# Attention burst of weighted values in two halves, and score maxima per PSUM bank

## The reference

```python
scores = jnp.einsum('bsqhd,bthd->bqhst', qh, kh) * scale
probs = jax.nn.softmax(scores, axis=-1)
a_dot = jnp.einsum('bqhst,bthd->bsqhd', probs, vh)
a_mem = sigma_q @ memory / (sigma_q @ memory_norm)   # sigma_q = elu(q)
out = a_dot * (1.0 - w) + a_mem * w
```

## Time and profile before

| | before |
|---|---|
| median of three runs | 767.34 us |
| profiled execution | 764.37 us |
| its span, first to last instruction | 762.6 us |
| PE busy | 705.8 us (93%) |
| DVE busy | 587.5 us (77%) |
| ACT busy | 486.2 us (64%) |
| POOL busy | 133.7 us (18%) |

### The profile page before, as it was taken

The page is one execution under the profiler, slowest core; times in us unless marked ns, Lnnn a source line. Parts: engine busy times, 40 slices in busy tenths (PEclk is TensorE's granted clock), DMA queues, the critical chain, the costliest instruction groups (busy, mean ns, idle before and its releaser), DMA issues.

```text
span 762.6 us, 14199 instructions
## 1 busy us (share of the span) xinstructions
PE 705.8 (93%) x3976; PEld 374.4 (49%) x3977; DVE 587.5 (77%) x800; ACT 486.2 (64%) x886; POOL 133.7 (18%) x282
## 2 busy tenths in 40 slices
PE   4999999898888888999988888899999999999998
PEld 2456544522222222221222212378888888888887
DVE  5366488899998899899899984377778777767754
ACT  1473600388888888888888878655665665556332
POOL 1000000666531111111111111010000000004750
PEclk9999999999999999999999999999999999999999
DMA  9729100187411110011110172042111111122431
GB/s 314 255 69 315 62 0 1 40 255 240 121 46 32 32 32 25 24 32 32 32 27 22 46 248 102 22 130 63 44 54 55 51 45 55 55 93 75 125 113 46
DMA packets 49951, 65.35 MB, mean 86 GB/s; under 512 B 8168, under 2 KB 42880, under 8 KB 49920
## 3 DMA queue, kind: packets, MB, share of 16 engines
q1 hardware_dynamic: 38560, 40.58, 16.8%
q10 hardware_dynamic: 8288, 15.99, 6.4%
q0 software_dynamic: 3072, 8.39, 3.5%
HBM read 40.15 MB, written 24.38 MB: 85 GB/s over the span
## 4 chain that ended last, share of the span: by engine, by line
PE 76%; ACT 11%; issue 5%; DVE 5%; ACTq 1%; DMA 1%; SPq 1%; POOL 0%; DVEq 0%; POOLq 0%
PE ps L1373 14%; PE ps L1402 14%; ACT att L736 10%; PE ps L1426 9%; PE ps L1472 9%; PE ps L1256 8%; PE ps L1506 6%; DVE smax L1006 4%; PE ps L1248 3%; PE ps L1521 3%; PE ps L1463 2%; PE ps L1216 2%; PE ps L1281 1%; PE ps L1362 1%; PE ps L1213 1%
## 5 line engine op out<-in xcount | busy, mean ns | idle before, releaser
L1006 DVE TENSOR_REDUCE smax<-ps 128x2 f32<-128x1024 f32 x256 | 302.4, 1221 | 33.6 <-PE ps L1281 30.5
L736 ACT ACTIVATE att<-ps 128x512 f32<-128x512 f32 x512 | 267.8, 602 | 53.6 <-PE ps L1426 50.8
L1426 PE MATMUL ps<-att 51*128 51x512 bf16 x512 | 165.4, 382 | 33.4 <-ACT att L736 21.0
L1281 PE MATMUL ps<-att 48*128 48x512 bf16 x512 | 163.0, 384 | 1.4 <-DVE smax L1006 1.4
L1426 PEld LDWEIGHTS ps<-att 51*128 51x128 bf16 x512 | 39.7, 93 | 200.9 <-ACT att L736 94.0
L1373 PE MATMUL ps<-att,v_head 128*32 128x512 f32 x1024 | 136.4, 604 | 1.7 <-ACT o_sb L695 0.6
L1402 PE MATMUL ps<-att_r 128*128 128x512 f32 x456 | 119.2, 410 | 2.8 <-DVE att_r L1067 2.8
L1063 DVE TENSOR_TENSOR att_r<-big,att_r 128x1024 fp32r<-128x1024 f32 x76 | 90.4, 1229 | 24.4 <-ACT att_r L716 23.8
L1402 PEld LDWEIGHTS ps<-att_r 128*128 128x128 f32 x456 | 86.7, 191 | 22.2 <-DVE att_r L1067 3.3
L716 ACT ACTIVATE att_r<-big 128x1024 fp32r x74 | 74.3, 1052 | 18.7 <-issue 18.7
L1472 PE MATMUL ps<-big,xn 128*128 x312 | 73.7, 380 | 0.0
(11 more groups left out here) (165 smaller groups left out, 697.0 us busy)
## 6 DMA issues: line engine op xcount, KB each, us to landing
big<-w ACTq DMA_DIRECT2D x8, 1024.0 KB
q_stacks<-big SPq DMA_DIRECT2D x12, 512.0 KB
att<-q_stacks SPq DMA_DIRECT2D x64, 96.0 KB, 2.1
slot_x<-zeros SPq DMA_DIRECT2D x1, 4992.0 KB, 17.1
e_x<-slot_x SPq DMA_DIRECT2D x39, 128.0 KB, 2.0
slot_y<-xn SPq DMA_DIRECT2D x39, 128.0 KB, 1.7
big<-w ACTq DMA_DIRECT2D x8, 512.0 KB
att<-k_stacks SPq DMA_DIRECT2D x64, 48.0 KB, 2.0
```

What stands on the lines that cost most here:

```text
L736: act.activation(probs[:, t % 2, g, :], ps[:, RING[turn_of(u) % 3], :], ACT.Exp, scale=SCALE)\
L1006: dve.reduce_max(smax[:, s % 2, :].rearrange("p (half v) -> p half v", half=2)[:, :, v], ps[:, bank:bank + 2, :], X_AXIS).then_inc(max_don ...
L1281: return pe.matmul(ps[:, bank + half, :], q_st[s][rows, g, P * st:P * (st + 1)], k_st[s][rows, :], start=True, stop=True)
L1426: pe.matmul(ps[:, RING[turn % 3], :], k_st[s][rows, P * t:P * (t + 1)], q_st[s][rows, g, :], start=True, stop=True).then_inc(scores_ready, 1)
```

## The change

The weighted values are split by their 512 queries into two parts of 256. The first part stands behind the quarter's first score pair (g = 0), the second behind the other one. The waits for the exponentials, for the values and for the copy of the previous outputs stand before the first part. The accumulation starts with part 0 and ends with part 1. The transposed outputs stand between the second pair and the second part.

The maxima are taken by two instructions for each tile, one for each bank, the bank of half 1 first, which is the one that PE writes first. Semaphores `a_ready` and `max_done` count banks, 16 per step, instead of tiles. On PE each `max_scores` matmul waits for its own bank. The hidden maxima of the shared stage do the same.

```diff
+        PART = SEQ // 2
...
-                pool.wait_ge(max_done, i * 8 + 8)
+                pool.wait_ge(max_done, i * 16 + 16)
...
 
             def maxima(i, s, v, bank):
 
-                dve.wait_ge(a_ready, i * 8 + (v + 1))
                 if v == 0:
                     wait(dve, m_ready, i - 1)
-                dve.reduce_max(smax[:, s % 2, :].rearrange("p (half v) -> p half v", half=2)[:, :, v],
-                               ps[:, bank:bank + 2, :], X_AXIS).then_inc(max_done, 1)
+                for half in (1, 0):
+                    dve.wait_ge(a_ready, i * 16 + (2 * v + 2 - half))
+                    dve.reduce_max(smax[:, s % 2, 8 * half + v:8 * half + v + 1], ps[:, bank + half, :], X_AXIS)\
+                       .then_inc(max_done, 1)
 
             res(1, kf, kr, kc[0])
 
...
                 bank = 2
                 if v == 0:
                     pe.wait_ge(stack_loaded[s], blk * 64 + 64)
-                wait(pe, max_done, i * 8 + v)
-                for half in range(2):
-                    last = max_scores(s, v, half, bank)
-                last.then_inc(a_ready, 1)
+                for half in (1, 0):
+                    wait(pe, max_done, i * 16 + (2 * v - half))
+                    max_scores(s, v, half, bank).then_inc(a_ready, 1)
 
             def max_scores(s, v, half, bank):
                 g, st = divmod(v, ST)
...
-                    pe.wait_ge(max_done, 16)
+                    pe.wait_ge(max_done, 32)
...
                                         o_sb[:, a, P * st:P * (st + 1)], ident[:, :])
                 last.then_inc(oT_in_psum, 1)
 
-            def weighted_values(i, s, t, pair=0):
-                pe.wait_ge(probs_ready, i * 16 + 4 * (t + 1))
-                if t == 0:
-                    pe.wait_ge(v_head_ready, i + 1)
-                    if s % 2 == 0:
-                        wait(pe, o_copied, pair)
+            def weighted_values(i, s, t, part, pair=0):
+
+
+                if part == 0:
+                    pe.wait_ge(probs_ready, i * 16 + 4 * (t + 1))
+                    if t == 0:
+                        pe.wait_ge(v_head_ready, i + 1)
+                        if s % 2 == 0:
+                            wait(pe, o_copied, pair)
+                queries = slice(PART * part, PART * (part + 1))
                 for g in range(G):
-                    last = pe.matmul(ps[32 * g:32 * (g + 1), 6, :], v_head[:, s % 2, t, :], probs[:, t % 2, g, :],
-                                     start=s % 2 == 0 and t == 0, stop=s % 2 == 1 and t == ST - 1)
-                last.then_inc(pv_done, 1)
+                    last = pe.matmul(ps[32 * g:32 * (g + 1), 6, queries], v_head[:, s % 2, t, :],
+                                     probs[:, t % 2, g, queries], start=s % 2 == 0 and t == 0 and part == 0,
+                                     stop=s % 2 == 1 and t == ST - 1 and part == 1)
+                if part == 1:
+                    last.then_inc(pv_done, 1)
 
             def transpose_x(j, pair, a):
                 pe.wait_ge(ex_loaded[a], pair * 16 + 16)
...
                             rows = slice(HALF * half, HALF * half + RM)
                             if not (last and turn - 3 == MAX_AT):
                                 bank_free(i, turn, pair if s % 2 == 0 else 0)
-                            if ahead and half == 0:
-                                if v == 0:
+                            if ahead:
+                                if v == 0 and half == 0:
                                     pe.wait_ge(stack_loaded[(s + 2) % 4], (blk + (s + 2) // 4) * 64 + 64)
-                                if isinstance(i, int) and i == 0 and v < 2:
+                                if isinstance(i, int) and i == 0 and v < 2 and half == 0:
                                     pe.wait_ge(mem_used, NT // 2 - 1 + v)
-                                wait(pe, max_done, (i + 2) * 8 + (v - 1))
+                                wait(pe, max_done, (i + 2) * 16 + (2 * v + half - 3))
                             pe.matmul(ps[:, RING[turn % 3], :], k_st[s][rows, P * t:P * (t + 1)],
                                       q_st[s][rows, g, :], start=True, stop=True).then_inc(scores_ready, 1)
                             if ahead:
-                                ins = max_scores((s + 2) % 4, v, 1 - half, 2 * (v % 2))
-                                if half == 1:
-                                    ins.then_inc(a_ready, 1)
-                    if t == OUT_AT // G - 1 and s % 2 == 0 and not first:
-                        transpose_o(pair - 1, (s // 2 + 1) % 2)
-
-                    if t > 0:
-                        weighted_values(i, s, t - 1, pair)
-                    elif not first:
-                        weighted_values(i - 1, s + 3, ST - 1)
+                                max_scores((s + 2) % 4, v, 1 - half, 2 * (v % 2)).then_inc(a_ready, 1)
+                        if t == OUT_AT // G - 1 and g == PAIR - 1 and s % 2 == 0 and not first:
+                            transpose_o(pair - 1, (s // 2 + 1) % 2)
+                        if t > 0:
+                            weighted_values(i, s, t - 1, g, pair)
+                        elif not first:
+                            weighted_values(i - 1, s + 3, ST - 1, g)
                     if t == MAX_AT // G - 1 and not last:
                         transpose_max(i + 1, s + 1)
 
...
                     step(blk, s)
             for i in range(STEPS - 4, STEPS):
                 step(NLOOP - 1, i % 4, ahead=i + 2 < STEPS, last=i == STEPS - 1)
-            weighted_values(STEPS - 1, STEPS - 1, ST - 1)
+            for part in range(2):
+                weighted_values(STEPS - 1, STEPS - 1, ST - 1, part)
             def transpose_h(j, a):
                 pe.wait_ge(h_ready, j + 1)
                 wait(pe, hT_ready, j)
```

## The result

Before and after in six runs each: 766.92 us (763.16 to 767.78) and 757.67 us (756.18 to 758.52). The ratio is 0.9882 [0.9864, 0.9901]: 9.25 us or 1.2% faster. The forecast was 757.6. The profiled execution of the kernel after took 757.83 us (span 755.7), 6.5 less than that of before; the latter lay 2.6 under its median, at a mean granted clock of 0.998. Of 35 executions of that kernel beside the experiments, the 15 at 0.998 took 764.2 to 766.0 us and the 18 at 0.993 to 0.996 took 766.3 to 769.1.

A forecast was written before the change was run, and what follows sets the result against it. A ring of PE and ACT was taken as the bound. Fourteen pairs at 0.66 (9.2) plus 0.9 less 0.4 gave 9.7 us: 764.37 to 754.7 profiled, 757.6 as median with 2.97 added; 8-in-10 range 747 to 771.

The forecast's parts named there:

- The ring: Ordinary quarter before: PE and ACT wait for each other, with the whole weighted-values block in the chain, 2.47 us a quarter.
- DVE 2.6 from being the bound: Pair of steps before: DVE's work makes 18.6 of 21.23 us, so DVE loses 2.6 us and does not bound.
- Half burst, 0.88: Weighted values on PE: 0.88 us between score pairs around one half, 0.25 of it per entry; PE's quarter 2.20 us.
- Reductions, 0.60 apart: Maxima on DVE: reductions of 512 elements 0.60 us apart, 0.06 of it the price of an instruction.
- The rival at 0.68: Neighbouring 512-element reductions on DVE do not overlap: pair 22.3 us, 782 us by the median; 9 in 100.
- What bank-wise maxima buy: A bank goes back to PE after 0.6 us instead of two after 1.13; 1.1 us more DVE work per pair.
- DVE's two stands, 0.55 and 0.29: Even steps: DVE runs dry 0.55 us at the wait for the output copy and 0.29 at the transposed outputs.
- Steps 30 and 31, 0.9: Last attention steps, without maxima: eight quarters gain 0.2 us each, less 0.7 for the wait that moved: 0.9 us gained.
- First steps and hidden maxima: Steps 0 and 1 already at DVE's pace: no gain; maxima hidden in the shared-expert stage: 0.4 us longer.
- The sum: Whole kernel: 9.2 us from fourteen pairs, plus 0.9, less 0.4, makes 9.7 us gained.
- The rival of the moved wait: First part waits for the output copy before two score pairs; 0.3 us longer chains keep pairs at 21.2: 767 us; 17 in 100.
- the rival of a complete cover: PE gets further ahead and DVE never stands: pair 19.73 us, 747 us in all; 13 in 100.

The follow-up runs named there:

- the first kernel: Weighted values split in two parts as in the changed kernel, but maxima by tile (one reduction of 1024 elements) as before: 757.53 us, ratio 0.990 against the kernel before.

## Why the prediction was right

The time and the direction were right, most durations to 0.05 us, and one credit was wrong. That the median came within 0.1 us of the forecast is luck.

- *The ring.* Right: taking some two fifths of DVE's reduction time out of the kernel before leaves its quarter at 2.47. "DVE 2.6 from being the bound" was too coarse, since that work cost 9 us outside the ordinary quarters.
- *Half burst, 0.88.* Measured 0.88; PE's quarter 2.20, measured 317.30 - 315.08 = 2.22. The 0.25 per entry holds for all three sizes.
- *Reductions, 0.60 apart.* Measured 0.598, so the price of an instruction is the 0.06 of the forecast. The rival at 0.68 had taken the length of one for the distance of two; they overlap. In the first kernel 16 of twice the size take 16 x 1.13 = 18.1 us a pair, here it is 32 x 0.598 = 19.1; the 1.0 goes against stands of every size, 2.2 us there and 20.67 - 19.1 - 0.53 = 1.0 here. The pairs differ by 0.12, and the two kernels take 757.5 and 757.7.
- *What bank-wise maxima buy.* Here the text was wrong: it counted them among what shortens the pair. Alone they bring nothing [0.9977, 1.0009], and nothing on top of the split while the copy's wait stands in front of it.
- *DVE's two stands, 0.55 and 0.29.* Measured 0.53 and 0.24, at the two places named and by the path named. T, the end of the odd step's 16th reduction, is 300.58 + 18 x 0.598 + 0.08 = 311.42. The first part came at T + 3.09 (forecast 3.03), DVE was dry at T + 3.59 (3.51) and restarted at T + 4.12 (4.06); it was dry again at T + 7.80 (7.66), until T + 8.03 (7.95). Their sum with 32 x 0.598 + 0.53 is 20.44; the pair takes 20.67. Most of the 0.2 left out is that a reduction in front of a stand has no neighbour to overlap with: the 32 take 14.43 + 3.68 + 1.21 = 19.32 and not 19.14. A gain of 0.56 per pair and not 0.66: 7.2 us over steps 2 to 29 for 9.2.
- *Steps 30 and 31, 0.9.* Measured 0.4. The 0.7 for the wait that moved, given without rows, is near the 0.97 - 0.19 = 0.78 that the stand grew by. But step 30 took 11.24, in part at a low clock (below); the first kernel, with a stand of 0.85 and the clock at 1.00, took 10.20.
- *First steps and hidden maxima.* Nothing and +0.4; measured -0.6 and +0.4. *After the attention* nothing was forecast, and it took 0.8 longer.
- *The sum.* 9.7 for the profiled executions; their spans differ by 6.9. The medians differ by 9.25, nearer to the forecast than its working earned: the profiled execution of before lay 2.6 under its median, and the forecast added 2.97 where 757.83 (mean clock 0.993) lies on the median of after.
- *The rival of the moved wait* was the right place to look. The forecast held that wait's cost (0.55 a pair) and took it for the price of the split. It is not: 11.5 us come back when the wait stands behind independent scores. That kernel's 746 is near the 747 of the rival of a complete cover, but not by its path: DVE still stands 0.27, and the pair is 19.99, not 19.73.

## What to carry to other kernels

A long block on an in-order engine that others wait behind is worth splitting while that engine has room for the extra entries (0.25 us each here: two parts gained 9 us, four lost 28). When a block is split, the wait in front of it moves up with its first part: see what is now queued behind it, and put independent work there first, since that cost more here than the split gained. Run each half of a joint change alone: here one of the two brought all of the gain that shows.

## What was not expected of the hardware

In step 30 of the changed kernel PE has no maxima to do and stands for the copy. Windows there (PE, PEld, DVE, ACT, POOL, granted clock, DMA):

```profile
458.00:460.00 2.00, 1.43 (x12) 0.39 (x11) 0.00 (x0) 1.95 (x6) 0.65 (x3) 1.00 0.98 399
460.00:461.00 1.00, 0.55 (x8) 0.19 (x8) 0.00 (x0) 0.80 (x2) 0.00 (x0) 0.93 1.03 376
...
462.00:463.00 1.00, 1.00 (x10) 0.10 (x2) 0.00 (x0) 0.85 (x2) 0.00 (x0) 0.50 0.00 0
...
465.00:466.00 1.00, 1.00 (x12) 0.34 (x10) 0.00 (x0) 1.00 (x3) 0.00 (x0) 1.00 0.07 16
```

PE was busy 1.43 of 2.0 us and 0.55 of the next, then the granted clock was 0.50 (1.2 GHz) for some 3 us, and back at 1.00 (2.4 GHz) by 465. The step took 11.24 us; with the wait moved back it took 9.76 at a granted clock of 1.00, and the first kernel, which has the copy's stand too, did it in 10.20 at 1.00. These are single profiles: such a stand is not always followed by a low clock.

The same happens where the mixture starts. PE stands 2.78 us there in both kernels, and then the granted clock is low for some 3 us before (first line) and some 7 us after (second line):

```profile
498.00:500.00 2.00, 2.00 (x6) 1.54 (x6) 1.59 (x2) 0.26 (x1) 1.92 (x2) 0.50 0.01 4
```

```profile
492.00:494.00 2.00, 2.00 (x7) 1.52 (x6) 1.67 (x1) 0.60 (x1) 0.59 (x1) 0.50 0.02 4
```

Over the profiles of all twelve kernels, what follows the attention takes 271.4 to 272.4 us without such a fall at its start, 272.8 to 273.6 with some 3 us of it, and 273.6 to 274.3 with some 7. So up to 3 us between two profiled spans need not come from their edits.
